# Cross attention: the last two mixing chunks of a turn copied by ScalarE instead of VectorE

## What is computed

```python
def _L0_xattn_ref(x, context, ...):          # x: [64, 32, 512], context: [64, 257, 512], 16 heads of 64
    xn = _layernorm(x, gamma, beta)
    q = (xn @ w_q).reshape(B, SQ, NUM_HEADS, DIM_HEAD)
    k, v = jnp.split(context @ w_kv, 2, axis=-1)
    scores = jnp.einsum('bqhd,bkhd->bhqk', q * SCALE, k)
    attn = jax.nn.softmax(scores, axis=-1)
    out = jnp.einsum('bhqk,bkhd->bqhd', attn, v).reshape(B, SQ, INNER)
    return (out @ w_out + b_out) * jnp.tanh(gate[0])
...
x = x + _L0_xattn_ref(_layernorm(x), ctx_1024, ...)
x = x + _L0_attn_ref(_layernorm(x), W_Q, W_K, W_V)      # attention within a token
x = x + _L0_ffn_ref(_layernorm(x), w_gate, w_up, w_down)
```

## Time and profile before

| | |
|---|---|
| median of 3 runs | 1829.09 us (1827.91 to 1829.17) |
| the profiled execution | 1831.52 us, its span 1829.7 us |
| TensorE matmul busy | 98% of the span |
| VectorE, ScalarE, GpSimd busy | 60%, 36%, 30% |
| cross attention, a middle turn | 62.9 us |
| mean granted TensorE clock | 0.994 of full speed |

### The profile page before, as it was taken

One profiled execution on the slowest core, in us unless ns is written; L12 is line 12 of the kernel. 1 busy time (PEld: TensorE's weight loads), 2 busy tenths in 40 slices (PEclk: granted clock), 3 DMA queues, 4 the chain that ended last, 5 costly groups with the idle time before them and its releaser, 6 DMA issues.

```text
span 1829.7 us, 38379 instructions
## 1 busy us (share of the span) xinstructions
PE 1794.3 (98%) x14608; PEld 1545.7 (84%) x14608; DVE 1104.6 (60%) x2271; ACT 666.8 (36%) x1356; POOL 557.9 (30%) x546
## 2 busy tenths in 40 slices
PE   5999999999999999999999999999999999999999
PEld 4888988998898899889988987788887878888887
DVE  6636566666756665666667566787888643333322
ACT  2245444545544454445445444311112411111111
POOL 3015434534444354345344444421121000000000
PEclk9999999999999999999999999999999999999999
DMA  7325444543554454445435538523440501010100
GB/s 254 127 97 145 123 109 125 139 133 90 146 137 116 114 150 123 107 127 140 133 90 145 137 105 237 160 78 96 126 139 13 180 6 69 1 69 0 46 1 23
DMA packets 236124, 199.23 MB, mean 109 GB/s; under 512 B 12896, under 2 KB 193376, under 8 KB 236064
## 3 DMA queue, kind: packets, MB, share of 16 engines
q1 hardware_dynamic: 231632, 189.74, 36.6%
q10 hardware_dynamic: 4432, 8.65, 1.3%
HBM read 130.98 MB, written 33.82 MB: 90 GB/s over the span
## 4 chain that ended last, share of the span: by engine, by line
PE 90%; DMA 1%; DVE 1%; SPq 0%; POOL 0%; issue 0%; ACT 0%; DVEq 0%; POOLq 0%; ACTq 0%
PE s_ps L83 25%; PE s_ps L84 24%; PE s_ps L85 24%; PE s_ps L579 7%; PE s_ps L634 6%; PE s_ps L641 1%; PE s_ps L1373 1%; PE s_ps L1387 1%; PE s_ps L1313 0%; PE s_ps L1398 0%; DMA a_xin<-x 0%; DMA a_m_xn<-x 0%; PE s_ps L588 0%; PE s_ps L1362 0%; DMA o_lo<-x_o_lo 0%
## 5 line engine op out<-in xcount | busy, mean ns | idle before, releaser
L83 PE MATMUL s_ps<-w_cT_hi,w_space_hi 128*128 128x258 f32 x1024 | 293.3, 286 | 0.2 <-DVE w_space_lo L725 0.2
L84 PE MATMUL s_ps<-w_cT_lo,w_space_hi 128*128 128x258 f32 x1024 | 289.9, 283 | 0.0
L85 PE MATMUL s_ps<-w_cT_hi,w_space_lo 128*128 128x258 f32 x1024 | 288.3, 282 | 0.0
L530 POOL TENSOR_TENSOR x_prob<-x_prob,x_share 128x256 f32<-128x256 f32 x256 | 156.0, 615 | 337.8 <-DVE x_share L692 329.9
L718 DVE COPY x_mix<-s_ps 128x512 f32<-128x512 f32 x256 | 174.5, 687 | 69.4 <-PE s_ps L85 67.0
L83 PE MATMUL s_ps<-x_pT_hi,x_cn_hi 128*128 128x512 f32 x512 | 206.3, 403 | 4.1 <-DVE x_mix L718 4.1
L850 ACT ACTIVATE x_prob<-s_ps,x_negmax 128x257 f32<-128x257 f32 x256 | 121.9, 476 | 240.9 <-DVE x_negmax L687 237.7
L85 PE MATMUL s_ps<-x_pT_hi,x_cn_lo 128*128 128x512 f32 x512 | 201.6, 394 | 0.0
L84 PE MATMUL s_ps<-x_pT_lo,x_cn_hi 128*128 128x512 f32 x512 | 200.9, 392 | 0.0
L83 PEld LDWEIGHTS s_ps<-w_cT_hi,w_space_hi 128*128 128x128 f32 x1024 | 193.4, 189 | 6.2 <-issue 3.8
L84 PEld LDWEIGHTS s_ps<-w_cT_lo,w_space_hi 128*128 128x128 f32 x1024 | 193.9, 189 | 0.7
(11 more groups left out here) (204 smaller groups left out, 3504.7 us busy)
## 6 DMA issues: line engine op xcount, KB each, us to landing
e_raw_T<-ctx_T SPq DMA_DIRECT2D x64, 514.0 KB, 4.7
e_raw_n<-ctx_nat SPq DMA_DIRECT2D x64, 512.0 KB, 4.1
x_prob_T<-x_blocks SPq DMA_DIRECT2D x256, 128.0 KB, 2.7
q<-q_q ACTq DMA_DIRECT2D x16, 512.0 KB, 2.8
e_q<-q SPq DMA_DIRECT2D x16, 512.0 KB, 4.1
o_hi<-x_o_hi SPq DMA_DIRECT2D x32, 256.0 KB, 3.3
o_lo<-x_o_lo SPq DMA_DIRECT2D x32, 256.0 KB, 3.8
a_oT_hi<-o_hi SPq DMA_DIRECT2D x16, 512.0 KB, 4.3
```

Of the source, the lines that this page charges most:

```text
L83: pe.matmul(out, lhs[0], rhs[0], start=start, stop=False)
L84: pe.matmul(out, lhs[0], rhs[1], start=False, stop=False)
L85: return pe.matmul(out, lhs[1], rhs[0], start=False, stop=stop)
L530: pool.tensor_tensor(prob[:, i, 0:KT * P], prob[:, i, 0:KT * P], share[:, i:i + 1].to_broadcast([P, KT * P]), ALU.mult)\
```

## The change

Chunks 2 and 3 of sample 3 are copied by ScalarE (line 909 of the changed kernel), on a semaphore of their own, `end_kept`, of two counts a turn; `mix_kept` counts two less. In the middle turns these copies stand on ScalarE behind `high_fold` of pair 5 and ahead of `high_T(t, 5)`; in the last turn behind the high probabilities and ahead of `w_high(range(RING))`. VectorE goes from the low half of fold 4 straight on to that of fold 5. In the last turn its four weight pieces, which stood one behind each copy, now stand together behind its two copies. The out projection waits for the first 14 counts of `mix_kept` and one of `end_kept` ahead of chunk 0, and for the second of `end_kept` ahead of chunk 3.

```diff
--- before.py
+++ after.py
@@ -377,7 +377,8 @@
     moved = s.count("moved", 16 * HT * GB)
     pT_hi, pT_lo = s.count("pT_hi", GB * KT), s.count("pT_lo", GB * KT)
     last_kept = s.count("last_kept", 1)
-    mixed, mix_kept = s.count("mixed", GB * DC), s.count("mix_kept", GB * DC)
+    mixed, mix_kept = s.count("mixed", GB * DC), s.count("mix_kept", GB * DC - 2)
+    end_kept = s.count("end_kept", 2)
     o_ready = s.count("o_ready", 2, 2)
     o_hi_done, o_lo_done = s.count("o_hi_done", 2), s.count("o_lo_done", 2, 2)
     o_stored = s.count("o_stored", 64, 32)
@@ -627,8 +628,11 @@
             for j in range(4 * m, 4 * m + 4):
                 out = [ps[h * HE:(h + 1) * HE, O_BANK[m], j % 4 * P:(j % 4 + 1) * P] for h in range(2)]
                 for c in range(DC):
-                    if j == 0:
-                        pe.wait_ge(mix_kept.sem, mix_kept.at(t, (GB - 1) * DC + max(c + 1, DC - 1)))
+                    if j == 0 and c == 0:
+                        pe.wait_ge(mix_kept.sem, mix_kept.at(t, GB * DC - 2))
+                        pe.wait_ge(end_kept.sem, end_kept.at(t, 1))
+                    if j == 0 and c == DC - 1:
+                        pe.wait_ge(end_kept.sem, end_kept.at(t, 2))
                     for h in range(2):
                         n = 2 * j + h
                         pe.matmul(out[h], w_v[:, c, n * HE:(n + 1) * HE], mix[:, c, :, place(n)],
@@ -799,11 +803,12 @@
             if more:
                 low_fold(t, 1, 3)
             for c in range(DC):
-                keep_mix(t, 3, c)
+                if c < 2:
+                    keep_mix(t, 3, c)
                 if more and c == 1:
                     low_fold(t, 1, 4)
-                elif not more:
-                    w_low(dve, range(2 * c + 1, 2 * c + 3, 2))
+            if not more:
+                w_low(dve, range(1, 2 * DC + 1, 2))
             if more:
                 low_fold(t, 1, 5)
             low_out(t, 0)
@@ -899,6 +904,10 @@
             if more:
                 for j in range(3, 6):
                     high_fold(t, 1, j)
+            for c in range(2, DC):
+                act.wait_ge(mixed.sem, mixed.at(t, 3 * DC + c + 1))
+                act.activation(mix[:, c, 3, :], ps[:, M_BANK[c % 2], :], ACT.Copy).then_inc(end_kept.sem, 1)
+            if more:
                 high_T(t, 5)
             else:
                 w_high(range(RING))
```

## The result

In 20 runs of each the changed kernel took 1832.05 us in the median (1830.19 to 1833.24), the kernel before 1828.66 us (1827.16 to 1831.06). The ratio is 1.0018, with a 95% interval of 1.0011 to 1.0025: 3.4 us more, 2.0 to 4.6 by the interval. The forecast was 3.9 us more.

The account below looks back on a forecast made before the run. TensorE, busy for 98% of the span, was taken as the bound. A last-turn cost of 5.3 us less 1.4 us gained in the turns gave +3.9 us: 1833.0 us on the median of 1829.09, range 1828.0 to 1837.0.

Parts of the forecast that it names:

- first stop of 0.36 us: Idle time before the out projection's first weight load; claimed to be no wait for the copy, so worth 0.
- second stop: Idle 0.22 us before the out projection's thirteenth weight load; claimed a wait for chunk 3's copy, 0.09 us shorter each turn.
- upper bound of 3.5 us: Most the 16 turns could gain if the whole 0.22 us wait for chunk 3's copy went; 1.4 us expected.
- rounding of the context 5 us later: Middle turns: ScalarE's rounding of the transposed context moves from 623.57 to 628.7, behind the copies; claimed cost 0.
- the landing of `o_lo`: Last turn: ScalarE may write `o_hi` again only after it; forecast at 1147.7 instead of 1142.64.
- the hand-over: Last turn into the next stage: late weight pieces delay its work; cost taken as 5.3 us, bounds 3.85 to 7.3.
- the third tile's input: Next stage: load issued after SyncE's six weight loads; claimed to have no cover and cost the full 5.05 us.
- Step 4: Next stage: TensorE's transposes of the first normalised tile move 3.85 us later; 5.9 us if the clock falls.
- The hidden hand-over: Rival, 0.18: the last turn's delay is covered and only the gain is left, 1827.7 or 1825.6 us.
- the gain of both stops: Rival, 0.07: both out projection stops are copy waits and go away, 8.9 us; 1825.5 us at most, 1820.2 if hidden.
- the clock as a separate case: Rival, 0.22: idle time ahead of the transposes halves TensorE's clock for 6.8 us of work; 1835.0, up to 1837 us.
- The sign of the slower side: Whole kernel: slower by over 0.2% given 0.52, within 0.2% given 0.40, faster given 0.08.

Follow-up runs that it names:

- e5_sem: Kernel before, VectorE still making all copies in the old order, but chunks 2 and 3 counted on end_kept: 1828.34 us, ratio 0.9996 to the kernel before.
- e6_T: Changed kernel, but in the middle turns the rounding of the transposed context stands ahead of ScalarE's two copies again: 1832.7 us, ratio 1.0020 to the kernel before.
- e4_four: Changed kernel, last turn: ScalarE rounds four weight pieces ahead of its copies, eight behind; VectorE's pieces between the copies: 1826.32 us, ratio 0.9987 to the kernel before.
- e8_queue: Changed kernel, but SyncE loads the second tile, mask, bias and gate ahead of the four weight loads waiting for slots: 1829.12 us, ratio 0.9999 to the kernel before.
- e7_bunched: Changed kernel, last turn: twelve weight pieces ahead of ScalarE's copies, VectorE's four pieces still behind each other: 1827.79 us, ratio 0.9993 to the kernel before.
- e3_twelve: Changed kernel, last turn: twelve weight pieces ahead of ScalarE's copies, VectorE's pieces between the chunks as before: 1826.23 us, ratio 0.9987 to the kernel before.
- e2_last: Changed kernel, but ScalarE copies chunks 2 and 3 in the last turn only, middle turns as before: 1835.03 us, ratio 1.0034 to the kernel before.
- e1_turns: Changed kernel, but ScalarE copies chunks 2 and 3 in the 15 middle turns only, last turn as before: 1827.3 us, ratio 0.9992 to the kernel before.

## Why the prediction was right

**What the copies cost and give in a turn.** I forecast 0.09 us a turn from a copy of 0.60 us in place of 0.69. The turns shortened by 0.094 us and the copies took 0.60. `e5_sem` rules out that the waits did it. That the first stop of 0.36 us is no wait for the copy was argued from one row of the last turn; it is now shown, since it stayed in all 16 turns put down to "issue", and in the middle turn above the copy was done 0.31 us before it began (625.17 against 625.84 - 0.36). Of the second stop I had expected 0.13 us to be left; the trace lists none, but one row of sixteen loads of 0.95 us. In the earlier trace rows the same sixteen took 1.05 us (from 628.07 to 628.92 + 0.20), and an unstopped group takes 0.91 us in the trace of `e5_sem` as in the change. So the real stop was 0.14 us of the listed 0.22, the rest being the ordinary distance of two such loads, and 0.04 us are left. My upper bound of 3.5 us for 16 turns was therefore too high; it was 2.2.

**The cover of the moved work.** The rounding of the context 5 us later was forecast at 0. `e6_T` takes it back and leaves the turn at 62.77 us.

**The last turn.** Counted from the start of the out projection, the steps came out so:

| step | forecast | measured |
|---|---|---|
| SyncE's fourth slot load ends | 5.14 | 5.24 |
| the gate's load is issued | 10.8 | 10.82 |
| `o_lo` is stored | 11.7 | 11.77 |
| ScalarE's second high half of `o` | 15.6 | 16.25 |
| GpSimd's root | 23.0 | 23.51 |
| transposes | 24.2 | 24.71 |
| third tile's input is issued | 29.6 | 29.82 |
| third tile's matmuls | 37.2 to 37.4 | 37.21 |

The one step half a microsecond off is the landing of `o_lo`: 4.5 us from its issue to the waiting row, where the trace before had 3.9. I forecast 5.3 us for the hand-over and 5.07 were measured, so the total of +3.9 us stands against 5.07 - 1.4 = +3.7 us in the traces (15 turns of 0.094 us lie ahead of the hand-over's start) and +3.4 us in the medians. `e4_four` shows that the delay comes with the pieces 0 to 3, and `e8_queue` that about half of it goes through SyncE's queue. `e7_bunched` removes 3.8 us by ScalarE's order alone, `e3_twelve` all of it with VectorE's order as well.

**The two ways to the end.** I expected the third tile's input to be what TensorE waits for, with the half clock just behind. In the trace it was TensorE that came last: it went from the second tile's transposes into the third tile's matmuls without a stop. The input had landed by 1164.38, when GpSimd used it, 0.5 us before. Counted from the out projection, that use came at 36.71 us, against 32.07 before (1164.18): the input's way cost 4.64 us and not 5.05, as the use came 6.9 us after the issue and not 7.5.

TensorE's own way was wrong by one term in the prediction. Step 4 gave it 3.85 us, or 5.9 with the lower clock, and set that beside the 5.05 us of the input. But in the kernel before TensorE had waited 0.92 us for this input, and so much of its own delay is covered; the same terms give 4.9 us. In the traces the transposes came 4.40 us later (24.71 against 20.31 us), the stretch from them to the end of TensorE's work was 1.6 us longer at the lower clock (12.50 against 10.91 us), and less 0.92 this is the 5.07 us. The 5.3 us that I took, somewhere between 5.05 and 5.9, came as near as it did partly by luck: the cover of 0.92 us was left out, the transposes came 0.55 us later than forecast, and the clock cost 0.4 us less than the 2 us I gave it.

Which way is last changes from run to run. TensorE was last in the change, in `e2_last` and by far in `e6_T` (39.03 us, 2.2 us behind what the input alone allowed); the input was last in `e8_queue`. In the trace of the change the clock thus put 0.4 us on top. How much of the mean loss the clock makes was not measured by itself: a kernel that keeps TensorE busy through the idle time was not tried.

**The rivals.** The hidden hand-over fell with `e2_last`; the gain of both stops fell with the row of 0.36 us; the clock as a separate case was half right, since it fell, but in the change all but 0.4 us of it ran beside the input's way and not on top of it. The sign of the slower side against "within 0.2%" was near even, and the measurement lies on that line: 1.0018.

## What to carry to other kernels

A step that is moved in a function that two kinds of turns share is two changes: here a saving of 0.09 us in each of 15 turns, and in the last one a delay of ten microseconds for what stands behind it in that engine's order. Ask of every new wait not what it waits for but what is queued behind it, and follow that through the queues that are in order as well, since about half of the loss came through SyncE's. And a listed stop is worth only what it has above the stop that the same change of matmuls shows without any wait.

## What the runs showed of the hardware

Before the runs I had taken a short idle time for harmless, as 1.41 us had left the clock alone. With 0.48 us ahead of the transposes (`e7_bunched`) and with 1.28 us (`e8_queue`), and the same 1.4 us behind them, the clock fell to 0.50, the 1.2 GHz level; in the five traces with nothing ahead of them (the kernel before, `e1_turns`, `e3_twelve`, `e4_four`, `e5_sem`) it stayed at 1.00. The stretches at the lower level lasted some 3 us in `e7_bunched` and `e8_queue`, 7 in the change and 10 in `e6_T`. The Trainium skill (TensorE: Matmul & The Clock Gate, "What's actually happening") has the lower clock as what the chip grants when TensorE has not been busy. The traces agree: each of these falls came behind idle time. What they add, with one or two executions for each case, is that half a microsecond more of idle time can be what brings it on.

VectorE and GpSimd, each with four weight pieces at once, came out at 1.6 and 1.7 us for a pair of one piece each (3.11 and 3.46 us for VectorE's two rows of two above), where 1.7 was forecast from single rows.
